# A two-layer graph kernel: shorter scale chains with a square root on ACT, an order for DVE in column 0, and b0 as one row

## The reference

```python
h = maximum(layernorm(x), 0)                      # eps 1e-5
x1 = swish((adj @ h) @ W0 + b0)
x  = x + swish((adj @ x1) @ W0 + b0)
h = maximum(layernorm(x), 0)
a_hat = adj + eye                                 # scaled by degree**-0.5 on both sides
x = x + (a_norm @ h) @ W1.T + b1
```

## Time and profile before

| what | value |
|---|---|
| median of 3 runs | 1433.33 us (1433.19 to 1433.46) |
| the profiled execution | 1431.94 us, its span 1430.1 us |
| TensorE busy | 1379.9 us, 96% |
| VectorE busy | 1062.2 us, 74% |
| ScalarE busy | 691.1 us, 48% |
| GpSimd busy | 61.4 us, 4% |
| TensorE's first matmul | 22.82 us after the start |
| ring loads of adj | 256 of 1024 KB |

### The profile page before, as it was taken

One profiled execution on the slowest core, in us unless ns is written; L12 is line 12 of the kernel. 1 busy time (PEld: TensorE's weight loads), 2 busy tenths in 40 slices (PEclk: granted clock), 3 DMA queues, 4 the chain that ended last, 5 costly groups with the idle time before them and its releaser, 6 DMA issues.

```text
span 1430.1 us, 18487 instructions
## 1 busy us (share of the span) xinstructions
PE 1379.9 (96%) x6598; PEld 649.7 (45%) x6598; DVE 1062.2 (74%) x2379; ACT 691.1 (48%) x797; POOL 61.4 (4%) x46
## 2 busy tenths in 40 slices
PE   3789999999999999999999999999999999999997
PEld 1334444444444444444444554454444444444443
DVE  7978777899999988977684767786766566656630
ACT  7886647888787676567640122222422332233200
POOL 1100000000010000000000011100000000000000
PEclk9999999999999999999999999999999999999999
DMA  9999999999999988797740111222543434343300
GB/s 378 381 423 409 386 410 387 422 420 418 403 392 393 375 339 322 317 381 302 314 168 30 52 45 67 67 67 89 192 181 154 187 141 190 148 188 137 140 22 17
DMA packets 58561, 352.28 MB, mean 246 GB/s; under 512 B 6496, under 2 KB 7008, under 8 KB 18528
## 3 DMA queue, kind: packets, MB, share of 16 engines
q1 hardware_dynamic: 51696, 339.11, 59.8%
q10 hardware_dynamic: 6768, 11.93, 2.2%
HBM read 339.21 MB, written 11.80 MB: 245 GB/s over the span
## 4 chain that ended last, share of the span: by engine, by line
PE 88%; DVE 5%; DMA 4%; ACT 2%; issue 1%; DVEq 0%; ACTq 0%; SPq 0%
PE acc_ps L720 21%; PE acc_ps L721 21%; PE acc_ps L656 12%; PE acc_ps L657 12%; PE early_ps L585 5%; PE early_ps L587 5%; DMA ring<-adj 3%; PE z_ps L568 3%; PE kept_ps L595 2%; PE kept_ps L596 2%; PE early_ps L626 1%; PE early_ps L625 1%; PE acc_ps L612 1%; PE acc_ps L613 1%; ACT marks L794 1%
## 5 line engine op out<-in xcount | busy, mean ns | idle before, releaser
L860 ACT ACTIVATE unused<-ring 128x2048 uint8<-128x2048 uint32 x204 | 389.4, 1909 | 71.5 <-DMA ring<-adj 62.6
L656 PE MATMUL acc_ps<-marks,node_a 128*128 128x512 fp8e4 x960 | 367.0, 382 | 41.3 <-DVE node_a L1001 32.0
L721 PE MATMUL acc_ps<-ring,node_a 128*128 128x512 fp8e4 x1024 | 388.1, 379 | 0.0
L720 PE MATMUL acc_ps<-ring,node_a 128*128 128x512 fp8e4 x1024 | 388.1, 379 | 0.0
L657 PE MATMUL acc_ps<-marks,node_a 128*128 128x512 fp8e4 x960 | 367.1, 382 | 0.0
L1008 DVE TENSOR_SCALAR marks<-ring 128x2048 uint8<-128x2048 f32 x226 | 280.7, 1242 | 75.0 <-DMA ring<-adj 37.6
L1294 DVE TENSOR_SCALAR_CACHE_REDUCE count_a<-marks 128x2048 uint8<-128x2048 f32 x52 | 118.8, 2284 | 114.4 <-DMA marks<-adj 112.7
L419 DVE TENSOR_SCALAR ring<-bits 128x256 uint32<-128x256 uint32 (+1 forms) x784 | 158.9, 278 | 40.0 <-PE acc_ps L721 39.8
L656 PEld LDWEIGHTS acc_ps<-marks,node_a 128*128 128x128 f16 x960 | 94.5, 98 | 162.1 <-issue 53.4
L721 PE MATMUL acc_ps<-ring,node_b 128*128 128x512 fp8e5 x416 | 157.7, 379 | 0.0
L720 PE MATMUL acc_ps<-ring,node_b 128*128 128x512 fp8e4 x416 | 157.7, 379 | 0.0
(11 more groups left out here) (129 smaller groups left out, 1229.1 us busy)
## 6 DMA issues: line engine op xcount, KB each, us to landing
ring<-adj SPq DMA_DIRECT2D x256, 1024.0 KB, 7.8
marks<-adj SPq DMA_DIRECT2D x52, 1024.0 KB, 5.4
node_b<-x SPq DMA_DIRECT2D x4, 1024.0 KB, 13.1
xch<-x SPq DMA_DIRECT2D x16, 256.0 KB, 2.7
xn_scratch<-xnew ACTq DMA_DIRECT2D x16, 256.0 KB, 2.0
xch<-xn_scratch SPq DMA_DIRECT2D x16, 256.0 KB, 2.9
out<-xnew ACTq DMA_DIRECT2D x16, 256.0 KB, 2.0
part_scratch<-stage ACTq DMA_DIRECT2D x13, 256.0 KB, 7.4
```

Source lines behind the costliest of these rows:

```text
L656: nc.tensor.matmul(acc_ps[c % 2][:, :], hi_of(node_a16, j), byte, start=(j == opens * TB), stop=False)
L720: nc.tensor.matmul(into[:, :], hi_of(node, j), byte.bitcast(E4), start=opens, stop=False)
L721: last = nc.tensor.matmul(into[:, :], lo_of(node, j), byte.bitcast(low), start=False, stop=closes)
L860: nc.scalar.activation(unused[:, :], loaded_slot(g).bitcast(U32), ACT.Sign, accum_out=nz_count[:, g:g + 1]).then_inc(counted, 1)
```

## The change

- Scales of x: three chains instead of four (`SCALED`: quarter 0, quarter 1, quarters 2 and 3 together). A chain is `spread_of` (4 steps on DVE), a square root on ACT (`root`), and `first_scales` (a reciprocal, one Newton round of three steps, and the mean's step).
- Column 0 on DVE is written out, not driven by the loop. Tiles 0 and 2 are marked by DVE, no longer by ACT. ACT's order changes with it: `make_h` stands behind the marks of tiles 1, 5, 7, 9 and 11.
- `feature_scales` takes its root from ACT, is six steps, and runs in one go after column 0's packing.
- b0 is loaded as one row into partition 0 of a block that POOL has cleared; a matmul with ones copies it to all partitions, and DVE takes it from there.

```diff
+SCALED = [(0, 16), (16, 16), (32, 32)]
-ACT_MARKED = [0, 1, 2, 3, 4, 5, 7, 9, 11, 13] + ...
+ACT_MARKED = [1, 3, 4, 5, 7, 9, 11, 13] + ...
-H_BEFORE = {1: (0, 1), 2: (2,), 6: (3,), 8: (4,), 10: (5,), 12: (6,), 14: (7,)}
+def spread_of(nc, link, stats, total, var, tmp, scale, ready):
+    st = stats.rearrange("p (j s) -> p j s", s=6)
+    tot = total.rearrange("p (j s) -> p j s", s=2)
+    link(nc.vector.tensor_tensor(tot, st[:, :, 1:3], st[:, :, 4:6], ALU.add))
+    link(nc.vector.tensor_tensor(tmp, st[:, :, 1], st[:, :, 4], ALU.subtract))
+    link(nc.vector.scalar_tensor_tensor(tmp, tmp, 0.25 * scale, tmp, ALU.mult, ALU.mult))
+    nc.vector.scalar_tensor_tensor(var, tot[:, :, 1], scale / D, tmp, ALU.mult, ALU.add).then_inc(ready, 1)
...
+            nc.gpsimd.memset(b_sb[:, 0:D], 0.0).then_inc(bias_zero, 1)
...
+                        nc.tensor.matmul(bias_ps, ones[:, :], b_sb[:, 0:D], start=True, stop=True).then_inc(wsum_done, 1)
...
-            act.dma_start(b_sb[:, 0:D], b0.to_broadcast([P, D])).then_inc(w_in, 16)
+            act.wait_ge(bias_zero, 1)
+            act.dma_start(b_sb[0:1, 0:D], b0).then_inc(w_in, 16)
...
+            def root(part):
+                a, n = SCALED[part]
+                act.wait_ge(var_ready, part + 1)
+                nc.scalar.activation(rstd[:, a:a + n], var[:, a:a + n], ACT.Sqrt, bias=eps_col[:, 0:1]).then_inc(root_ready, 1)
...
+            root(0)
+            make_h(0)
+            make_h(1)
+            root(1)
             for e in ORDER:
+                    if g == 5:
+                        root(2)
...
                     if g in ACT_MARKED:
                         act_mark(e)
-                    for part in H_BEFORE.get(g + 1, ()):
-                        make_h(part)
+                    if g == 1:
+                        make_h(2)
+                        make_h(3)
+                    if g in (5, 7, 9, 11):
+                        make_h((g + 3) // 2)
+                    if g == 13:
+                        act.wait_ge(wsum_done, 1)
+                        nc.scalar.activation(bound, wsum_ps, ACT.Sqrt).then_inc(bound_rooted, 1)
...
+                link(nc.vector.reciprocal(r, r))
+                link(nc.vector.scalar_tensor_tensor(t, r, -0.5, r, ALU.mult, ALU.mult))
+                link(nc.vector.scalar_tensor_tensor(t, v, EPS * H_SCALE ** -2, t, ALU.add, ALU.mult))
+                link(nc.vector.scalar_tensor_tensor(r, t, 1.5, r, ALU.add, ALU.mult))
...
+            def feature_scales():
...
+                link(nc.vector.tensor_copy(b_sb[:, 0:D], bias_ps))
+                link(nc.vector.scalar_tensor_tensor(wtmp, b_sb[:, 0:D], -1.0, b_sb[:, 0:D], ALU.mult, ALU.max))
+                link(nc.vector.scalar_tensor_tensor(bound, bound, SUM_BOUND, wtmp, ALU.mult, ALU.add))
...
-            for part in range(2):
-                first_stats(part)
-                first_rest(part)
...
+            first_stats(0)
+            first_spread(0)
+            first_scales(0)
+            mark(ORDER[0])
+            first_stats(1)
+            first_spread(1)
+            h_low(0)
+            first_scales(1)
+            h_low(1)
+            first_stats(2)
+            mark(ORDER[2])
+            h_low(2)
+            first_stats(3)
+            first_spread(2)
+            pack_half(0)
+            first_scales(2)
+            mark(ORDER[6])
+            h_low(3)
+            pack_again(0)
+            pack_last(0)
+            h_low(4)
+            mark(ORDER[8])
+            pack_half(1)
...
+            h_low(5)
+            mark(ORDER[10])
+            pack_again(1)
+            pack_last(1)
...
+            h_low(6)
+            mark(ORDER[12])
+            pack_half(2)
+            h_low(7)
+            mark(ORDER[14])
+            mark(ORDER[15])
+            pack_again(2)
+            pack_last(2)
+            feature_scales()
```

More of the change, by code:

```diff
@@ L52 @@
 NORM_PARTS = [16, 16, 16, 16]
+SCALED = [(0, 16), (16, 16), (32, 32)]
+SCALED_QUARTERS = [1, 2, 4]
 H_PART = 8
@@ L59 @@
 COUNT_STEPS = 11
-FEATURE_STEPS = 18
-ACT_MARKED = [0, 1, 2, 3, 4, 5, 7, 9, 11, 13] + [TC + i for i in range(1, TC, 2)] + [g for g in range(2 * TC, 5 * TC) if g % 4 == 3]
+ACT_MARKED = [1, 3, 4, 5, 7, 9, 11, 13] + [TC + i for i in range(1, TC, 2)] + [g for g in range(2 * TC, 5 * TC) if g % 4 == 3]
 AHEAD = {2 * TC + 7: (13, 14), 2 * TC + 11: (11, 12), 3 * TC + 7: (9, 10), 3 * TC + 11: (7, 8)}
@@ L68 @@
 FIRST_AHEAD = min(AHEAD_COLUMNS)
-LATE = list(range(TC)) + ACT_MARKED[10:] + [c * TC + i for c in sorted(AHEAD_COLUMNS) for i in range(2)]
+LATE = list(range(TC)) + [g for g in ACT_MARKED if g >= TC] + [c * TC + i for c in sorted(AHEAD_COLUMNS) for i in range(2)]
 LATE_STEP = 4
-H_BEFORE = {1: (0, 1), 2: (2,), 6: (3,), 8: (4,), 10: (5,), 12: (6,), 14: (7,)}
 class Entry:
@@ L671, in _ @@
                         pe.wait_ge(wsq_ready, 1)
-                        nc.tensor.matmul(wsum_ps, ones[:, :], wsq, start=True, stop=True).then_inc(wsum_done, 1)
+                        nc.tensor.matmul(wsum_ps, ones[:, :], wsq, start=True, stop=True)
+                        nc.tensor.matmul(bias_ps, ones[:, :], b_sb[:, 0:D], start=True, stop=True).then_inc(wsum_done, 1)
                     if c == 1 and i == 6:
@@ L811, in make_h @@
                 first = part * H_PART
-                act.wait_ge(ln_ready, 1 + [sum(NORM_PARTS[:q + 1]) > first for q in range(len(NORM_PARTS))].index(True))
+                act.wait_ge(ln_ready, 1 + [a + n > first for a, n in SCALED].index(True))
                 for j in range(first, first + H_PART):
@@ L994, in first_stats, with first_spread, first_scales @@
                 norm_stats(ln_stat, x_in[part], sum(NORM_PARTS[:part]), NORM_PARTS[part])
-            def first_rest(part):
-                norm_rest((ln_stat, ln_step, ln_ready), part, sum(NORM_PARTS[:part]), NORM_PARTS[part], H_SCALE)
+            def first_spread(part):
+                a, n = SCALED[part]
+                dve.wait_ge(ln_stat, SCALED_QUARTERS[part])
+                spread_of(nc, chain(dve, ln_step, 7 * part), stats[:, a * 6:(a + n) * 6], mv[:, a * 2:(a + n) * 2],
+                          var[:, a:a + n], tmp[:, a:a + n], H_SCALE ** -2, var_ready)
+            def first_scales(part):
+                a, n = SCALED[part]
+                v, r, t = var[:, a:a + n], rstd[:, a:a + n], tmp[:, a:a + n]
+                dve.wait_ge(var_ready, part + 1)
+                dve.wait_ge(root_ready, part + 1)
+                link = chain(dve, ln_step, 7 * part + 3)
+                link(nc.vector.reciprocal(r, r))
+                link(nc.vector.scalar_tensor_tensor(t, r, -0.5, r, ALU.mult, ALU.mult))
+                link(nc.vector.scalar_tensor_tensor(t, v, EPS * H_SCALE ** -2, t, ALU.add, ALU.mult))
+                link(nc.vector.scalar_tensor_tensor(r, t, 1.5, r, ALU.add, ALU.mult))
+                twice_mean = mv[:, a * 2:(a + n) * 2].rearrange("p (j s) -> p j s", s=2)[:, :, 0]
+                nc.vector.scalar_tensor_tensor(nmr[:, a:a + n], twice_mean, -0.5, r, ALU.mult, ALU.mult).then_inc(ln_ready, 1)
             def h_low(part):
@@ L1115, in low_part @@
                                                ALU.mult, ALU.subtract).then_inc(node_ready, 1)
[L1117 to L1147, removed]
@@ new lines, in feature_scales @@
+            def feature_scales():
+                link = chain(dve, bound_step, 0)
+                dve.wait_ge(wsum_done, 1)
+                dve.wait_ge(bound_rooted, 1)
+                link(nc.vector.tensor_copy(b_sb[:, 0:D], bias_ps))
+                link(nc.vector.scalar_tensor_tensor(wtmp, b_sb[:, 0:D], -1.0, b_sb[:, 0:D], ALU.mult, ALU.max))
+                link(nc.vector.scalar_tensor_tensor(bound, bound, SUM_BOUND, wtmp, ALU.mult, ALU.add))
+                link(nc.vector.tensor_scalar(bound, bound, 1e-18, None, ALU.max))
+                link(nc.vector.tensor_scalar(bound.bitcast(I32), bound.bitcast(I32), 0x7F800000, None, ALU.bitwise_and))
+                nc.vector.tensor_scalar(s_row[:, :].bitcast(I32), bound.bitcast(I32), -1.0, float((127 + 127 + 14) << 23),
+                                        ALU.mult, ALU.add).then_inc(s_ready, 1)
+                dve.wait_ge(s_ready, 1)
@@ L1160, in _ @@
             nc.vector.memset(first_row[0:1, :], 1.0).then_inc(ones_set, 1)
-            for part in range(2):
-                first_stats(part)
-                first_rest(part)
-            for e in ORDER:
+            nc.vector.memset(eps_col[:, :], EPS * H_SCALE ** -2).then_inc(eps_set, 1)
+            first_stats(0)
[6 more added lines that the diff above has]
+            first_scales(1)
@@ new lines, in _ @@
+            h_low(1)
[13 more added lines that the diff above has]
+            pack_half(1)
+            dve.wait_ge(w_in, 32)
+            nc.vector.tensor_tensor(wsq, w_sb[:, 0:D], w_sb[:, 0:D], ALU.mult).then_inc(wsq_ready, 1)
@@ L1166, in _ @@
+            for e in ORDER[TC:]:
                     c, i, g = e.c, e.i, e.g
```

(7 more changed lines are left out.)

12 lines of the change are left out of this document (8 added, 4 removed).

## The result

The changed kernel takes 1431.39 us (median of 20 runs, 1429.94 to 1433.31), the kernel before 1433.37 (20 runs, 1432.18 to 1436.08): ratio 0.9988, 95% interval 0.9982 to 0.9993. It is faster, by 2.0 us (1.0 to 2.6 by the ends of the interval), not by the 4.5 forecast. The time is inside the range; the gain is less than half of the forecast one, and under the 2.87 us that the prediction asked for before it would say "faster".

A forecast was written before the change was run, and what follows sets the result against it. TensorE is full from 120 us, so the end follows the DMA stream's shortfall by some 105 us. Sum: 1.30 + 3.48 - 0.3 = 4.5 us off 1433.33, giving 1428.8; range 1427.2 to 1431.8.

The forecast's parts named there:

- They move only as a block: TensorE's last 1310 us, from 120 us on, are fixed matmul work; the end moves as much as its waiting ends earlier.
- Between tile 24 and tile 35 nothing changes: In that stretch all work hangs on arrivals and DVE and ACT have room, so no gain or loss was expected.
- b0's row, 1.30 us: Loading b0 as one row removes the stream's hole at 6.5 to 9.5 us; all tiles arrive 1.3 us earlier.
- rival A: b0's packets are not the first hole's cause; b0's row is worth only 0.2 us, end 1429.8; chance 0.14.
- The two holes: DMA stream short of 424 GB/s at 6.5 to 9.5 us (1.30 us) and 50 to 70 us (3.48), together 4.78.
- The chains and the order, 3.48 us: Shorter scale chains and new order relieve full DVE, so marks come in time and the hole at 50 to 70 us goes.
- The 0.3 us for ACT: Taken off the gain because ACT in column 0 is late next, by a hair, and further slip would cost the stream.
- the room of 0.7 us: Column 0: the nearest of ACT's marks clears by 0.7 us the 2.7 us needed before the tile three places behind lands.
- Rival B: ACT bounds column 0, slipping 1.5 to 3 us; 1 to 2.5 us of hole return, end 1430 to 1431.5; chance 0.17.
- root 2: ACT's square root for the third scale chain in column 0, forecast just in time at 30.1 to 30.4 us.
- rival C: Square roots bring up to 7 more ACT table loads before tile 16; 8.3 us lost against 4.8 won, 1436.8; chance 0.05.
- the forecast 0.6 us for mark 2: Column 0: DVE's mark of tile 2 beside POOL's copy at 23.2 us would slip 0.6 us if the shared ports lock.

The follow-up runs named there:

- e2: Kernel before with only b0's load changed: one row, a matmul with ones and a DVE copy; 1433.29 us, ratio 1.0001 (0.9992 to 1.0010).
- the three pairs: e3 against the changed kernel, f2 against f1 (the early root's second run), e5 against e4: b0 copied takes 0.15 us more in the mean.
- e3: Changed kernel with b0 loaded as before, copied to 128 partitions by the load, without the extra matmul and DVE copy; 1430.41 us, ratio 0.9987.
- e5: e4 with b0 loaded as in the kernel before, copied to 128 partitions by the load; 1429.85 us, ratio 0.9975.
- f2: The early root with b0 loaded as in the kernel before, copied to 128 partitions by the load; 1430.04 us, ratio 0.9982.
- The early root: Changed kernel with an extra square root ahead of ACT's wait for the first scales; 1429.31 and 1429.48 us, ratios 0.9975 and 0.9979.
- e4: The early root, with tile 7 marked by DVE instead of ACT and tile 2 marked ahead of the third statistics; 1429.91 us, ratio 0.9971.
- f3: Repeat of e6: e4 with tile 79, the last of column 4, marked by DVE instead of ACT; 1430.42 us, ratio 0.9983.
- e6: e4 with tile 79, the last of column 4, marked by DVE instead of ACT; 1429.55 us, ratio 0.9974.

## Why the prediction was right in sign and wrong in size

- **The bound.** "They move only as a block" holds in the means (a lead of 2.9 us at 128 us, a gain of 3.0 in the medians), but not tile by tile: the windows of 20.00 out of 20 us held for the kernel before because TensorE came to no tile before its mark was there, and with TensorE ahead it waited at 269.35 us with the stream at full rate. "Between tile 24 and tile 35 nothing changes" failed: from 80 to 100 us, 1.1 us of the lead was lost in the first trace.
- **b0's row, 1.30 us.** b0's load was the cause of the hole (412 to 434 GB/s in its place, in all nine traces with b0 as a row), rival A is out. The term was not right: by e2's interval the row gains at most 1.1 us, and by the three pairs it is worth 0.15 us (-0.4 to 0.7). The two holes were added, "1.30 + 3.48", though a lead of 1.3 us at 10 us is kept only if the marks that free the slots come early enough for it. The 125 ns a packet were no price either: in e3, e5 and f2 the hole is the same (246 to 251 GB/s) and the packets take 36, 50 and 84 ns.
- **The chains and the order, 3.48 us.** The hole from 50 to 70 us went whole, as stepped out. The durations were right: the reciprocal took 0.25 (0.21 taken), the root 0.31 (0.3). The times slipped behind the first root: mark 14 ended at 55.6 (forecast 54.3), mark 16 started at 60.02 (58.5).
- **The 0.3 us for ACT.** This is the term that was mis-sized most: 2.2 to 2.6 us in three traces. Of the slip, 1.3 to 1.5 us came in at the very first root, twice the room of 0.7 us. Rival B, "ACT becomes the bound of column 0", is the nearest to what happened, and its 1 to 2.5 us of hole coming back is the size that the traces show. Half of it was not root 2 or the low parts but the table load behind a wait: I counted the loads (two, right; rival C is out) and didn't ask where the first would stand. The early root gives back 1.15 us of time. The other 1.1 to 1.3 us from 15 to 50 us stay with the load early; marks moved to DVE took 0.3 to 0.9 of them (413, 416 and 420 GB/s in e4, f3 and e6), and why marks at their forecast times still cost the stream that much stays open.
- **What was taken from pages.** The Trainium skill on the table sets (ScalarE: Activation LUTs, Table sets: the hidden batching unit) held for relu and copy, and sign, which it doesn't name, ran beside the root too: no trace has a third load. For one load the Trainium skill (ScalarE: Activation LUTs, What ACT_TABLE_LOAD costs) has 1283 ns, and 1380 ns more for draining the engine; the trace has 1.28 us, and the root starts 0.02 us after it. On the ports shared by DVE and POOL (the Trainium skill, SBUF — State Buffer, SBUF: two separate sides) the forecast 0.6 us for mark 2 was 0.1: it took 1.35 us beside POOL's copy at 24.57 instead of 1.22. The Trainium skill has the lock in that section for VectorE's operations with two inputs in SBUF, or in a two-port mode; no run shows whether a mark is one of them.
- **The sum anew.** By the first trace: 1.3 + 3.5 - 2.6 = 2.2 us at 75 us; 1.4 to 2.5 at 128 us in three traces, 2.0 in the medians. The time fell inside the range because the range made room for rival B (1430 to 1431.5); the sum itself was off by more than half.

## What to carry to other kernels

When an engine takes over a function that needs a table, issue a dummy of it before the first wait for data: here the load then stood where the engine was idle, and behind the wait it was on the path. Don't add gains of two holes in one transfer stream: fill the second by rerunning the schedule with the new arrival times, and look for the engine whose marks or frees then come late. An engine that is busy for a whole window tells nothing of the room that its feeder has; look there too before you count on a lead. And when you follow a lead by traces, ask how quick the trace is that you measure from: a quick one makes every lead seem to shrink.

## What the runs showed of the hardware

- A load that reads one 512 B row for 128 partitions is dear for the others. From 6.5 to 9.5 us the stream beside it ran at 240, 246, 248 and 251 GB/s in four kernels, and at 412 to 434 in the nine traces with the row loaded once. The time of its own packets doesn't tell the price: 125 ns each in the kernel before, but 0.069 x 48 us / 93 = 36 ns in e3, with the same hole. How they hold up the stream stays open. As one row the small queue's 142 packets from 2.5 to 6 us took 6.3% of 16 engines, 25 ns each. The first line is e3's from 6.5 to 9.5 us, the second the changed kernel's from 2.5 to 6:

```profile
q10 hardware_dynamic: 93, 0.04, 6.9%
...
q10 hardware_dynamic: 142, 0.06, 6.3%
```

- The stall without a releaser is at 117.23 in the kernel before and at 115.38 after, and one fp32 matmul, two instructions in the trace, was added at tile 9. It keeps its place in the instructions: in these two, in e2 and in e3 it stands behind the 330th matmul instruction of the trace. In all four, one packet of 16 KB of an instruction queue is under way from 110 to 118 us, 0.8% of 16 engines for 8 us, 1.0 us on one engine:

```profile
q8 instruction: 1, 0.02, 0.8%
```

That it is TensorE waiting for instructions is argued from this, not shown. The Trainium skill, Runtime: NRT & Kernel Launch (Instruction fetch mechanics), has blocks of 16 KiB fetched while the engine works, with a cost that is mostly hidden; if the stall is such a fetch, 0.7 to 1.7 us of it were not hidden in the traces of these kernels.

- Single executions of one kernel spread by 4 us and more here (1429.12 to 1433.31 for the changed one over its three sets, 1431.31 to 1437.34 for the kernel before in one set). In the traces a part of it is seen as waits of 0.2 to 1.4 us for single marks between 128 and 392 us. One trace is good for a mechanism and its place, not for a microsecond at the end.
